# Attention with values as weights: the result transposed in two column tiles, probabilities normalised before they are transposed

## What is computed

```python
k_all = k_blocks[block_tables]...          # the new k and v are written into the blocks first
v_all = v_blocks[block_tables]...
qg = q.reshape(Bx, G, GSZ, Tx, HD)         # GSZ = 2 heads share one group's k and v
scores = jnp.einsum('bghtd,bgsd->bghts', qg, k_all) * SCALE
scores = jnp.where(allowed[:, None, None, :, :], scores, -jnp.inf)
p = jax.nn.softmax(scores, axis=-1)
o = jnp.einsum('bghts,bgsd->bghtd', p, v_all).reshape(Bx, H, Tx, HD)
o = o.transpose(0, 2, 1, 3).reshape(Bx, Tx, H * HD)
return jnp.einsum('bto,do->btd', o, Wo)
```

## Time and profile before

| | us |
|---|---|
| median of 3 runs | 1115.25 (1112.25 to 1119.34) |
| the profiled execution | 1114.8 |
| its span, first to last instruction | 1111.8 |
| TensorE busy in the span | 981.9 (88%) |
| VectorE busy | 528.1 (48%) |
| ScalarE busy | 407.0 (37%) |
| GpSimd (POOL) busy | 303.7 (27%) |
| mean granted TensorE clock | 0.933 |

### The profile page before, as it was taken

The page is one execution under the profiler, slowest core; times in us unless marked ns, Lnnn a source line. Parts: engine busy times, 40 slices in busy tenths (PEclk is TensorE's granted clock), DMA queues, the critical chain, the costliest instruction groups (busy, mean ns, idle before and its releaser), DMA issues.

```text
span 1111.8 us, 18526 instructions
## 1 busy us (share of the span) xinstructions
PE 981.9 (88%) x5042; PEld 688.6 (62%) x5043; DVE 528.1 (48%) x2080; ACT 407.0 (37%) x1204; POOL 303.7 (27%) x250
## 2 busy tenths in 40 slices
PE   5999958899999999819889996999199999999994
PEld 2464357677777777714344445887177777777772
DVE  5768882544555788532334441555323333333331
ACT  3424312555656556401111111222154444555540
POOL 3000132266555341111333431223212221211221
PEclk9989955899999999968999998999599999999998
DMA  8765560334544554148776754993733334333430
GB/s 273 234 228 197 186 209 22 96 76 127 163 141 114 174 157 133 58 120 231 213 216 124 138 105 151 338 380 115 232 92 57 60 66 74 67 64 69 73 48 0
DMA packets 82422, 156.31 MB, mean 141 GB/s; under 512 B 16023, under 2 KB 28999, under 8 KB 80768
## 3 DMA queue, kind: packets, MB, share of 16 engines
q1 hardware_dynamic: 38160, 84.87, 23.5%
q0 software_dynamic: 25520, 45.11, 19.8%
q10 hardware_dynamic: 18688, 25.71, 7.3%
HBM read 94.05 MB, written 73.19 MB: 150 GB/s over the span
## 4 chain that ended last, share of the span: by engine, by line
PE 59%; DVE 15%; DMA 11%; issue 8%; DVEq 3%; ACT 2%; SPq 1%; POOL 0%; ACTq 0%; POOLq 0%
PE ps L628 41%; PE ps L709 7%; DMA acc<-R,tok_i 5%; PE ps L634 4%; PE ps L699 3%; DMA R<-acc 3%; PE ps L692 3%; DMA rows<-zrow 1%; DVE R L1346 1%; DVE R L1338 1%; DVE R L1356 1%; DMA R<-rows 1%; DVE R L1349 1%; ACT R L994 1%; ACT R L978 1%
## 5 line engine op out<-in xcount | busy, mean ns | idle before, releaser
L628 PE MATMUL ps<-R 128*128 128x128 f32 (+4 forms) x2768 | 680.7, 403 | 20.6 <-DMA R<-in_x_t 11.4
L628 PEld LDWEIGHTS ps<-R 128*128 128x128 f32 x2768 | 420.8, 194 | 243.2 <-issue 219.6
L634 PE MATMUL ps<-ident,R 128*128 128x128 f32 x504 | 77.3, 285 | 62.7 <-DMA R<-rows 50.1
L600 POOL DMA_INDIRECT out_x<-R,tok_i x39 | 60.9, 1562 | 253.7 <-DVEq L1781 165.6
L634 PEld LDWEIGHTS ps<-ident,R 128*128 128x128 f32 x504 | 62.1, 149 | 91.7 <-issue 75.6
L526 POOL DMA_INDIRECT rows<-R,slot_i x64 | 65.8, 1027 | 178.4 <-DVEq L1533 95.7
L709 PEld LDWEIGHTS ps<-R 128*128 128x128 f32 x768 | 94.9, 196 | 20.2 <-ACT R L994 19.0
L709 PE MATMUL ps<-R 128*128 128x64 f32 x768 | 98.0, 279 | 5.0 <-ACT R L994 5.0
L1422 DVE CUSTOM_DVE_ANT_0 R<-ps,R 128x384 f32<-128x384 f32 x128 | 66.0, 554 | 74.8 <-issue 74.7
L988 ACT ACTIVATE R<-R,nmx 128x384 f32<-128x384 f32 x128 | 77.5, 607 | 54.7 <-DVE nmx L1422 54.5
L600 POOL DMA_INDIRECT acc<-R,tok_i x39 | 60.6, 1554 | 125.2 <-DVE R L1690 120.1
(11 more groups left out here) (280 smaller groups left out, 900.8 us busy)
## 6 DMA issues: line engine op xcount, KB each, us to landing
R<-rows SPq DMA_DIRECT2D x78, 258.0 KB, 3.4
R<-in_fc ACTq DMA_DIRECT2D x16, 1024.0 KB, 7.2
m_buf<-R SPq DMA_DIRECT2D x8, 1024.0 KB, 5.1
R<-m_buf SPq DMA_DIRECT2D x16, 512.0 KB, 4.2
R<-acc SPq DMA_DIRECT2D x32, 256.0 KB, 5.5
new_kv<-R SPq DMA_DIRECT2D x16, 256.0 KB, 2.1
qn<-R SPq DMA_DIRECT2D x16, 256.0 KB, 2.5
R<-qn SPq DMA_DIRECT2D x8, 512.0 KB, 3.8
```

Source lines behind the costliest of these rows:

```text
L600: po.indirect_dma_start(out=sums[s], out_offset=bass.IndirectOffsetOnAxis(ap=tok_i[:, s:s + 1], axis=0), in_=y_sb[s], in_offset=None, boun ...
L628: m = pe.matmul(out, lhs(k), rhs(k), start=(k == 0 and first), stop=(k == KC - 1 and last))
L634: m = pe.transpose(out[:, k * P:(k + 1) * P], src[:, k * P:(k + 1) * P], ident[:])
```

## The change

The value product is turned round: v, 128 keys x 64 features, is the weights, and the transposed probabilities of two heads, 128 keys x 256, move. The result is o transposed, features in partitions. The two groups of a half go to partitions 0 to 63 and 64 to 127 of bank 1, that is two column tiles of 64. One `mix` serves four units: 3 chunks x 2 tiles, 12 passes. A period has four of them, in slots 3, 5, 7 and the next slot 1.

Since tokens now lie in columns, the row sums can't be applied to the result. `scale` on VectorE multiplies the probabilities by the reciprocal sums ahead of their transposes: for each pair one reciprocal and two TENSOR_SCALARs of 128 x 384 in place, before the next slot's `tops`; `turn_p` waits for it (`s_sc`) and no longer for `expo`. `norm`, `o_sb`, `tail` and their two uses of bank 0 go. `o_out` copies bank 1 to one of two `o_t`, in slots 2 and 6 (`s_ot`). `prob_t` is two buffers of four units. The "h0" half moves from slot 1 to 2, the q1 turn from 4 to 1 in mid periods, and POOL's wait is counted in new units.

The features of o come in another order, so w_o is loaded by eight DMAs of 64 rows, and the gate is folded into Wo in two column tiles of 64: 16 more products of 8 columns, 32 more passes.

```diff
+        prob_t = [words(R2, base, [4, NJ // P - 1, P]) for base in (7424, 14336)]
-        o_sb = words(R2, 10496, [D])
-        o_t = words(R2, 11008, [KC, P])
+        o_t = [words(R2, base, [KC, P]) for base in (10240, 15872)]
...
-                "mid": ("a0", "h0", "o1", "a1", "h1", "q1", "q0", "o0", "k0", "k1", "rt"),
+                "mid": ("a0", "q1", "h0", "a1", "h1", "q0", "k0", "k1", "rt"),
...
-                    sp.dma_start(w_o[:, :, 0:D], d["wo_t"].rearrange(chunked, p=P)).then_inc(S["att_w"], 16)
+                    for k in range(KC):
+                        for x in range(2):
+                            row = HD * (4 * (k // 2) + 2 * x + k % 2)
+                            sp.dma_start(w_o[HD * x:HD * (x + 1), k, 0:D], d["wo_t"][row:row + HD, :]).then_inc(S["att_w"], 16)
...
-                    po.wait_ge(S["s_pv"], 16 * b)
+                    po.wait_ge(S["s_pv"], 4 * b)
...
-                chunks(ps[:, 7, k * NE:(k + 1) * NE], lambda o: raw_wo[:, o, k * P:(k + 1) * P], lambda o: gate0[:, o, :])
+                for x in range(2):
+                    col = HD * (4 * (k // 2) + 2 * x + k % 2)
+                    chunks(ps[HD * x:HD * (x + 1), 7, k * NE:(k + 1) * NE], lambda o: raw_wo[:, o, col:col + HD], lambda o: gate0[:, o, :])
...
             def turn_p(B, u):
-                wait(pe, S["s_exp"], 16 * B + u + 1)
+                wait(pe, S["s_sc"], 16 * B + u + 1)
...
-            def mix(B, u, s):
-                qt, h = u // NH, HEADS[u % NH]
-                wait(pe, S["s_pe"], 16 * B + u + 1)
-                if u % NH == 0:
-                    wait(pe, S["s_norm"], 2 * B + qt)
+            def mix(B, m, s):
+                qt = m // 2
+                wait(pe, S["s_pe"], 16 * B + 4 * m + 4)
+                if m % 2 == 0:
+                    wait(pe, S["s_ot"], 2 * B + qt)
                 for c in range(3):
-                    m = pe.matmul(ps[:, 1, h * HD:(h + 1) * HD], prob_t[u % 4][:, c * P:(c + 1) * P],
-                                  kv[s][:, qt + c, (NG + h // 2) * HD:(NG + h // 2 + 1) * HD], start=(c == 0), stop=(c == 2))
-                m.then_inc(S["s_pv"], 1)
+                    for x in range(2):
+                        g = NG + 2 * (m % 2) + x
+                        n = pe.matmul(ps[HD * x:HD * (x + 1), 1, KC // 2 * P * (m % 2):KC // 2 * P * (m % 2 + 1)].rearrange("p (i q) -> p i q", q=P),
+                                      kv[s][:, qt + c, g * HD:(g + 1) * HD], prob_t[m % 2][:, x::2, c, :], start=(c == 0), stop=(c == 2))
+                n.then_inc(S["s_pv"], 1)
...
+                    if j == 1 and mid:
+                        pe.wait_ge(S["q_ld"], 16 * (B + 2))
+                        turn_q(at, 1)
...
                     if j == 1 and not first:
-                        project(at, "h0")
+                        mix(B - 1, 3, 1 - s)
+                    if j in (3, 5, 7):
+                        mix(B, (j - 3) // 2, s)
...
-            def o_out(at, x):
-                out_of(at["o" + x], o_t.rearrange(flat))
+            def o_out(B, qt, read):
+                wait(ac, bk, read)
+                wait(ac, S["s_pv"], 4 * B + 2 * qt + 2)
+                copy_bank(1, o_t[qt].rearrange(flat)).then_inc(S["s_ot"], 1)
...
-            def norm(B, qt):
+            def scale(B, j):
+                v = 2 * j
+                wait(ve, S["s_exp"], 16 * B + v + 2)
+                ve.reciprocal(rsum[:, v % NH:v % NH + 2], sums[:, v:v + 2])
+                ve.drain()
+                for u in (v, v + 1):
+                    TS(prob[u % 4], prob[u % 4], rsum[:, u % NH:u % NH + 1], None, ALU.mult).then_inc(S["s_sc"], 1)
...
                 for j in range(NH):
+                    if j or not first:
+                        scale(B if j else B - 1, (j - 1) % NH)
                     tops(B, j)
```

More of the change, by code:

```diff
@@ L274, in wait @@
                 eng.wait_ge(semaphore, value)
-        USES = {"first": ("ct", "q1", "q0", "k0", "k1", "o0"),
-                "mid": ("a0", "h0", "o1", "a1", "h1", "q1", "q0", "o0", "k0", "k1", "rt"),
-                "last": ("a0", "h0", "o1", "a1", "h1", "o0", "rt", "a2"),
-                "after": ("h2", "o1", "rt")}
+        USES = {"first": ("ct", "q1", "q0", "k0", "k1"),
+                "mid": ("a0", "q1", "h0", "a1", "h1", "q0", "k0", "k1", "rt"),
+                "last": ("a0", "h0", "a1", "h1", "rt", "a2"),
+                "after": ("h2", "rt")}
         NF, NM, NL = (len(USES[k]) for k in ("first", "mid", "last"))
@@ L747, in period @@
                     if j == 0 and not first:
-                        wait(pe, bc, at["a0"] - 1)
+                        wait(pe, bc, at["a0"] - (B > 1))
                     dots(B, j, s)
                     if j == 0 and not first:
-                        project(at, "a0")
+                        project(at, "a0", 2 * B - 1)
+                    if j == 1 and mid:
+                        pe.wait_ge(S["q_ld"], 16 * (B + 2))
+                        turn_q(at, 1)
                     if j == 2 and first:
                         cell_sums(at)
+                    if j == 2 and not first:
+                        project(at, "h0", 2 * B - 1)
                     if j == 3 and not first:
-                        project(at, "a1")
+                        project(at, "a1", 2 * B)
+                    if j == 4 and first:
+                        pe.wait_ge(S["q_ld"], 16 * (B + 2))
+                        turn_q(at, 1)
                     if j == 4 and not first:
-                        project(at, "h1")
-                    if j == 6:
-                        if not first:
-                            tail(at, "0", 2 * B + 1)
-                    if j == 6 and first:
-                        pe.wait_ge(S2["kvd"][1 - s], 64)
+                        project(at, "h1", 2 * B)
+                    if j == 5 and not last:
+                        turn_q(at, 0)
+                    if j == 6 and not last:
+                        pe.wait_ge(S2["kvd"][1 - s], 64 * ((B + 1) // 2 + 1))
                         turn_k(at, 0, 1 - s)
-                    if j == 7 and first:
-                        tail(at, "0", 2 * B + 1)
-                    if j == 7 and mid:
+                    if j == 7 and not last:
                         turn_k(at, 1, 1 - s)
@@ L1008, in period @@
                 for j in range(NH):
[L1009 to L1010 removed]
+                    if j == 1 and mid:
+                        q_out(at, 1, 1 - s)
+                    if j == 2 and not first:
+                        o_out(B - 1, 1, uses(B - 1, "mid")["h1"] + 1 if B > 1 else 0)
+                    if j == 4 and first:
+                        q_out(at, 1, 1 - s)
                     if j == 5 and not last:
[L1012 removed]
+                        q_out(at, 0, 1 - s)
+                    if j == 6:
+                        o_out(B, 0, at["h0"] + 1 if not first else 0)
                     if j == 6 and not last:
[L1014 to L1019 removed]
                         k_out(at, 0, 1 - s)
@@ L1022, in period @@
                         k_out(at, 1, 1 - s)
-                    if j == 7 and first:
-                        o_out(at, "0")
                     for u in (2 * j, 2 * j + 1):
@@ L1039, in _ @@
             evac(NB - 1, 15)
-            o_out(uses(NB, "after"), "1")
+            o_out(NB - 1, 1, uses(NB - 1, "last")["h1"] + 1)
             ac.wait_ge(S["e_lg"], 1)
@@ L1585, in period @@
                         row_low(at, "a0", 2 * B - 2)
-                    if j == 1 and not first:
-                        norm(B - 1, 1)
-                        row_high(at, "h0", 2 * B - 2, 0)
                     if j == 2:
@@ L1592, in period @@
                         first_cells()
+                    if j == 2 and not first:
+                        row_high(at, "h0", 2 * B - 2, 0)
                     if j == 3 and first:
@@ L1602, in period @@
                         row_high(at, "h1", 2 * B - 1, 1)
-                    if j == 5:
-                        norm(B, 0)
                     if j == 5 and not first:
@@ L1643, in _ @@
             at = uses(NB, "after")
+            scale(NB - 1, NH - 1)
             row_high(at, "h2", NT - 2, 0)
-            norm(NB - 1, 1)
             ve.wait_ge(S["e_in"], 1)
```

68 lines of the change are left out of this document (13 added, 55 removed).

## The result

The changed kernel took 1106.35 us (median of 14 runs; 13 of them 1099.72 to 1110.12, and one of 1389.31, at a mean granted clock of 0.669, stands apart) against 1116.05 (1110.43 to 1123.57, 14 runs) for the kernel before: ratio 0.9901, 95% interval 0.9878 to 0.9924. That is 1% faster, 10 us, where 22 were forecast. The profiled execution has a span of 1105.8 us (before 1111.8) and a mean granted clock of 0.925 (before 0.933).

A forecast was written before the change was run, and what follows sets the result against it. TensorE was taken to bound B = 1 to 4, with VectorE not far behind in B = 5 to 7. From 1114.8 us, +1.2 - 2.5 - 17 + 0.4 - 1.5 - 2.5 = -21.9 gave 1093; range 1084 to 1112.

The forecast's parts named there:

- Column tiles side by side: Value products: the two column tiles overlap, 1.55 us for four units, ends 1.45 and 2.75.
- take turns: Value products: column tiles do not overlap, four units cost 2.75 us as before; total 1111; chance 18%.
- their loads lie open: Value products: each pair of passes waits for its weights, 0.65 us more in 16 places; total 1103; chance 7%.
- TensorE's period: B = 1 to 4: 28.3 us of work and 1.4 of waits, period 29.7, gain 5.0.
- POOL is next: B = 1 to 4: POOL's loop, 31.9 us its own, takes back 3 us (0 to 6), leaving -17.
- 2 us of slack: B = 1 to 4: margin of 2 us left between POOL's gathered rows landing and TensorE's key turn wanting them.
- the forecast's own range: Whole kernel: 1085 to 1102 us for the main case, chance 58%, spread by POOL, gate and waits.
- B = 5 to 7: Attention periods bound by VectorE, about 35.5 us: +0.4 for B = 5 and 6, -1.5 for B = 7.
- VectorE slower than priced: Attention periods: TENSOR_SCALAR at the PSUM row's rate, 0.20 us more, 16 in a period; total 1108; chance 10%.
- B = 0: First attention period: a pair of value products goes, TensorE waits longer behind `move_cells`; -2.5 us.
- The end of the stage: After B = 7: a pair of value products, norm and an o turn go, a scale comes; -2.5 us.
- Gate and w_o: Before the attention stage: eight tiling changes +1.2 us; eight w_o DMAs put 3.2 us on SP's queue, costing 0.

The follow-up runs named there:

- swapped loops: Changed kernel with the acc DMAs sent early, and all six value passes of one column tile before the other's six: 1096.31 us, ratio 0.9859.
- early burst: Changed kernel with SP's sixteen acc DMAs sent together at about 178 us, not four at a time in B = 0 to 3: 1089.11 us.
- the repeat: The changed kernel measured again as it is, for a second profile: 1104.57 us.
- gathers first: Changed kernel with POOL's sends and next-period gathers ahead of all seven scatter-adds of the period: 1128.85 us, ratio 1.0107.

## Why the prediction was off

**Column tiles side by side: right.** 1.45 us against 1.55 for four units; the rivals in which they take turns, or in which their loads lie open, fall. In the Trainium skill, "TensorE: Matmul & The Clock Gate", section "The mechanism", one sentence has a load overlap a running matmul only where the row groups differ, while another also lets it go ahead into the background weight buffer. Here all weights span the same 128 rows, and 12 passes of 0.23 us with 1.06 us of loads (PEld) end in 1.45: the trace doesn't agree with the first sentence. The prediction's own row against loads in the open, 0.107 us for a pass of the full array, proved nothing, since it took the whole pass as the load; the load records of line 709 do: 192 ns at the median, one every 107.

**TensorE's period: right.** 29.2 to 29.5 us in B = 1 to 4 where neither POOL nor the swapped loops bind, against 29.7, and the 20 us for B = 1 to 4 are there in the early burst (20.5).

**"POOL is next": the step that failed.** It was named, and sized at 3 us where it takes 12 to 19 (20.5 less the 8.2 and 1.5 that the two profiles kept). The working gave the loop 31.9 us of its own, 5.1 of them the late scatter-add, and had that one "give some of it back". From one gather of old rows to the next, the loop took:

| kernel | loops from B = 1 to 4, us |
|---|---|
| before | 34.1, 34.7, 34.7 |
| changed | 34.8, 34.0, 32.8 |
| changed, once more | 34.7, 32.0, 34.7 |
| changed, gate as before | 34.6, 33.3, 34.4 |
| changed, early burst | 30.2, 30.2, 31.1 |

The nine loops with the burst in its old place have a mean of 33.9, two more than the 31.9. Where they come from shows in one loop of each kernel, the one of the earlier trace rows and the one from 269.11 to 303.14 above, cut at the third scatter-add behind the gather (308.38 and 281.25) and three scatter-adds further on (321.98 and 296.31):

```profile
308.38 1.62 POOL L534 DMA_INDIRECT m_buf<-tot,cell_i  x1 [0.30 <-issue]
...
315.30 1.57 POOL L534 DMA_INDIRECT m_buf<-tot,cell_i  x1 [0.70 <-DMA m_buf<-tot,cell_i]
...
331.41 1.01 POOL L503 DMA_INDIRECT R<-in_kv_pool,old_idx  x1 [1.60 <-PE ps L709]
```

| stretch of the loop | before | after | difference |
|---|---|---|---|
| gather to third scatter-add | 11.66 | 12.14 | +0.48 |
| over the burst, three scatter-adds on | 13.60 | 15.06 | +1.46 |
| from there to the next gather | 9.43 | 6.83 | -2.60 |

The last stretch held the waits for VectorE and TensorE, 1.80 and 1.30 more than an issue. Of these 3.10 us the loop did lose 2.60: taking them off was nearly right, and only 0.5 came back (0.3 as waiting for a scatter-add to land, 0.2 in an issue of 1.76 instead of 1.56 us). What filled the gap is mostly the burst, the half of the step that went the other way. Over B = 1 to 3, the scatter-add that meets the burst was followed by the next after 7.6, 6.9 and 6.7 us before, and after 9.2, 8.4 and 7.7 in the changed kernel. Before, it was issued 0.6 to 0.9 us ahead of SP's first DMA to acc; after, 1.1 to 2.5 us behind it. In the repeat, the loop of 32.0 us is the one whose scatter-add was issued 1.4 us ahead of the burst; in the other two it was 0.3 and 1.1 us behind, and the next followed after 9.5. That this order makes the difference is not shown: no run moved one against the other alone. That the burst makes the length is shown by moving it. The first stretch grew because POOL's issues themselves took longer: the seventeen of a loop are busy 21.1 us before and 21.4 to 21.9 in loops of changed kernels, the early burst among them. Whether VectorE's new work beside them is the reason, no run tells.

The step also counted on 2 us of slack. They were gone at the first: POOL came to its gather 9.9 us into B = 1 (9.2 in the repeat), where with the early burst, waiting for TensorE, it came 6.7 us in.

**The range held, for the wrong reason**: 1106.35 lies in 1084 to 1112, but the forecast's own range ended at 1102, and the case that came true, POOL's loop as the bound, had no rival of its own; to a time within 1% of the kernel before, which is what came (0.9901), it gave 0.29. With the loop put at 34 us, afterwards, the same sum gives +1.2 - 2.5 - 2.8 + 0.4 - 1.5 - 2.5 = -7.7, so 1107; that this meets the 1106.35 is partly luck, since the terms for the start, B = 0 and the end didn't come as taken (below).

**B = 5 to 7: right in kind.** TENSOR_SCALAR was to be 0.41 us and is 0.433. The periods were to be 35.5, with VectorE busy over 33; it is busy 31.93 and 32.35, and in the profiles of changed kernels with the adds on VectorE the periods are 33.7 to 37.1, mostly 34 to 35 (gathers first aside, whose cells come late), so near the bound, with no gain that counts. "VectorE slower than priced" falls.

**B = 0: the work right, the clock not foreseen.** B = 0 was to lose 2.5 us. It took 46.0 to 46.7 us in the three profiles with the old value product, at a mean granted clock of 0.70 to 0.72. In two of the changed kernels' profiles the clock was 0.71 and 0.72, and B = 0 took 43.5 and 43.4, 2.5 to 3.3 less. In seven others (tile by tile left out) it was 0.65 to 0.67, and B = 0 took 46.5 to 47.5. So the work that was saved is mostly lost again in a lower clock. TensorE's wait for the scale behind `move_cells` grew too, from 4.79 to 5.88, but it is 5.70 in one of the short ones as well. Why the clock differs, the runs don't show.

**The end of the stage: too much.** B = 7 and the end took 45.4 to 46.5 us in the changed kernels with all adds on VectorE, against 47.0 to 48.5, so about -1.5 and not -4.0.

**Gate and w_o: nothing that can be measured**, where +1.2 was taken. No run shows the 1.2 us. The eight DMAs took 4.97 us of SP's queue, 4.5 more than the one, rather than 3.2; the start of the stage doesn't show it.

## What to carry to other kernels

When one engine gets faster by 15% in a stretch, walk through the next engine's loop at the new period, with the transfers that will then stand beside it, and give "it is the bound" a case of its own. A wait inside such a loop can mostly be taken off (2.6 of 3.1 us here); what its transfers meet at their new places can cost as much again. A burst of plain DMAs is worth placing where no chain of dependent transfers is open; here the same 16 DMAs, moved, turned 1% into 2.1%, and did nothing for the kernel in which the loop was covered.

## What the runs showed of the hardware

- Column tiles of float32 passes overlap, and how well depends on the order of issue: 1.45 us alternating, 1.93 tile by tile, for 12 passes of 256 columns.
- An indirect DMA that adds in memory and waits for the landing of the one before follows it after 3.1 to 3.4 us where nothing else is in the way; across a 2 MB burst the wait is 4.8 to 7.9 us instead of 1.7.
- POOL's elementwise work held up VectorE's where both work on SBUF (4.05 us for an add of 1.09, 2.99 for two scales of 0.75), while VectorE's `tops`, with one input in PSUM, kept its 0.55 us.
- The granted clock of the same stretch differs from one execution to the next, and the time goes with it: B = 0 of the changed kernel took 43.4 and 43.5 us at a mean granted clock of 0.72 and 0.71, and 46.5 to 47.5 at 0.65 to 0.67.
